# Attention over an adjacency mask, fp32 by two parts: 20 of 128 transposed probability blocks per batch taken from TensorE to VectorE squares and a DMA placement

## The reference

```python
h = jnp.maximum(_layernorm(x, axis=-1), 0.0)          # x: (16, 1024, 512)
q = (h @ Wq + bq).reshape(b, n, H, HD)                # H = 8 heads of HD = 64
k = (h @ Wk + bk).reshape(b, n, H, HD)
v = (h @ Wv + bv).reshape(b, n, H, HD)
scores = jnp.einsum('bihd,bjhd->bhij', q, k) / jnp.sqrt(jnp.float32(HD))
mask = jnp.where(adj == 0, jnp.float32(-1000000000.0), jnp.float32(0.0))
weights = jax.nn.softmax(scores + mask[None, None, :, :], axis=-1)
out = jnp.einsum('bhij,bjhd->bihd', weights, v)
return x + out.reshape(b, n, H * HD)
```

## Time and profile before

| | |
|---|---|
| median of 3 runs | 3952.41 us (3952.12 to 3953.52) |
| profiled execution, its time | 3952.87 us |
| its span | 3951.1 us |
| TensorE matmul busy | 3925.2 us, 99% |
| TensorE weight load busy | 3219.8 us, 81% |
| VectorE busy | 3109.3 us, 79% |
| ScalarE busy | 3010.7 us, 76% |
| GpSimd busy | 1389.6 us, 35% |
| granted TensorE clock | 0.999 |

### The profile page before, as it was taken

The page is one execution under the profiler, slowest core; times in us unless marked ns, Lnnn a source line. Parts: engine busy times, 40 slices in busy tenths (PEclk is TensorE's granted clock), DMA queues, the critical chain, the costliest instruction groups (busy, mean ns, idle before and its releaser), DMA issues.

```text
span 3951.1 us, 64302 instructions
## 1 busy us (share of the span) xinstructions
PE 3925.2 (99%) x21504; PEld 3219.8 (81%) x21504; DVE 3109.3 (79%) x5263; ACT 3010.7 (76%) x5386; POOL 1389.6 (35%) x1399
## 2 busy tenths in 40 slices
PE   8999999999999999999999999999999999999998
PEld 7888888888888888888888888888888888888887
DVE  7878878788787887878878788787887868878687
ACT  6877868778686886868868688686886868868687
POOL 4334333343333333333333333333333333334322
PEclk9999999999999999999999999999999999999999
DMA  6233333333323333334233342332433324324232
GB/s 208 60 88 72 88 78 67 85 79 80 83 66 83 89 70 84 73 75 95 63 84 80 68 96 65 82 84 62 96 73 75 87 61 94 80 67 90 51 76 49
DMA packets 722325, 316.44 MB, mean 80 GB/s; under 512 B 629840, under 2 KB 629840, under 8 KB 713424
## 3 DMA queue, kind: packets, MB, share of 16 engines
q1 hardware_dynamic: 722000, 312.34, 34.7%
HBM read 173.28 MB, written 38.27 MB: 54 GB/s over the span
## 4 chain that ended last, share of the span: by engine, by line
PE 92%; DVE 6%; issue 1%; ACT 1%; POOL 0%; DMA 0%; ACTq 0%; POOLq 0%; DVEq 0%
PE T L604 21%; PE misc L558 16%; PE S L589 11%; PE O L623 11%; PE S L590 11%; PE O L616 11%; PE misc L571 9%; DVE pT L909 2%; DVE S L903 1%; PE misc L537 1%; DVE bn L869 1%; DVE qB L886 1%; DVE y L928 0%; DVE qA L886 0%; ACT pT L722 0%
## 5 line engine op out<-in xcount | busy, mean ns | idle before, releaser
L909 DVE TENSOR_TENSOR pT<-T,pT 128x512 fp32r<-128x512 f32 x2048 | 1378.7, 686 | 657.1 <-ACT pT L722 651.5
L722 ACT CAST pT<-T 128x512 fp32r<-128x512 f32 x2048 | 1187.1, 590 | 412.8 <-PE T L604 326.1
L903 DVE CUSTOM_DVE_ANT_0 S<-S,mask 128x1024 f32<-128x1024 f32 x1024 | 1251.9, 1223 | 1.2 <-PE S L590 1.2
L604 PEld LDWEIGHTS T<-ident,probs 128*128 128x128 f32 x8192 | 996.9, 140 | 301.8 <-DVE pT L909 64.4
L604 PE MATMUL T<-ident,probs 128*128 128x128 f32 x8192 | 1236.5, 273 | 4.6 <-DVE pT L909 0.5
L741 ACT ACTIVATE probs<-S,negmax 128x1024 f32<-128x1024 f32 x1024 | 1150.7, 1124 | 7.0 <-DVE negmax L903 3.8
L623 PE MATMUL O<-pT,vs 128*64 128x512 f32 x2048 | 954.5, 466 | 0.2 <-DVE pT L909 0.2
L616 PE MATMUL O<-pT,vs 128*128 128x512 f32 x2048 | 816.1, 398 | 0.0
L558 PE MATMUL misc<-hT,wqk 128*128 128x512 f32 x3036 | 734.3, 391 | 0.0
L456 POOL TENSOR_TENSOR outs<-outs,oT 64x512 f32<-64x512 f32 x255 | 338.2, 1326 | 1024.4 <-DMA outs<-oT 1021.1
L558 PEld LDWEIGHTS misc<-hT,wqk 128*128 128x128 f32 x3036 | 570.0, 188 | 122.0 <-issue 0.2
(11 more groups left out here) (78 smaller groups left out, 3298.9 us busy)
## 6 DMA issues: line engine op xcount, KB each, us to landing
wqk<-wqk_split SPq DMA_DIRECT2D x63, 1024.0 KB, 6.0
xln<-in_x SPq DMA_DIRECT2D x240, 256.0 KB, 2.7
kA<-kA SPq DMA_DIRECT2D x128, 256.0 KB, 3.2
kB<-kB SPq DMA_DIRECT2D x128, 256.0 KB, 3.8
outs<-in_x SPq DMA_DIRECT2D x256, 128.0 KB, 3.6
outs<-oT SPq DMA_DIRECT2D x256, 128.0 KB, 3.6
out<-outs SPq DMA_DIRECT2D x252, 128.0 KB, 3.3
rinv_sq<-rinv_turned SPq DMA_DIRECT2D x512, 2.0 KB, 1.7
```

Of the source, the lines that this page charges most:

```text
L604: mm = pe.transpose(T[:, u % 2, i * P:(i + 1) * P], probs[:, (GB * g + i) % RING, j * P:(j + 1) * P], ident[:])
L722: act.copy(pT[:, u % PT, 0, :], T[:, u % 2, :]).then_inc(p_hi, 1)
L903: dve.tensor_tensor_reduce(S[:, s % 2, :], S[:, s % 2, :], mask[:, s % NB, :], 1.0, 3.0e38, ALU.add, ALU.min, negmax[:, s % RING:s % RING ...
L909: dve.tensor_tensor(pT[:, u % PT, 1, :], T[:, u % 2, :], pT[:, u % PT, 0, :].bitcast(F32), ALU.subtract).then_inc(p_lo, 1)
```

## The change

Twenty units of a batch are no longer turned by TensorE. Two neighbouring units make a pack: `PACKS` lists for ten packs the slot in which VectorE turns it (`at`) and its first unit (`slot`), always four later. One VectorE transpose (`turn_pack`) turns 128 x 256 columns of four ring slots in squares of 32x32 into a buffer (`squares`: part of `wv`, or `xln` for the packs from slot 121 on). As squares stay on their own 32 partitions, SP stores them to DRAM with four DMAs, one for each 32 partitions (`store_pack`, slot `at`), and one slot later, when all four have landed, loads them with two DMAs, one a unit, to the right partitions, into the place in `probs` that the unit came from (`load_pack`). `probs_hi` and `probs_low` of such a unit read `probs` in place of T, and `probs_hi` waits for the load. On ScalarE it stands behind the slot's exponential. The high half of wv that the squares overwrite is kept in DRAM (`wv_dram`) and loaded again in slot 110 (`load_wv`). The slots of the statistics of x go from (5, 7, 11, 13, 37, 39, 43, 45) to (5, 7, 11, 37, 39, 43, 69, 71). In the last batch only packs with `at` under 96 are moved.

```diff
--- before.py
+++ after.py
@@ -70,7 +70,7 @@
 HT_AT = {s: t for t, s in enumerate(HT_SLOTS)}
 NORM_AT = {s - 2: t for t, s in enumerate(HT_SLOTS)}
-STATS_SLOTS = (5, 7, 11, 13, 37, 39, 43, 45)
+STATS_SLOTS = (5, 7, 11, 37, 39, 43, 69, 71)
 STATS_AT = {s: t for t, s in enumerate(STATS_SLOTS)}
 COPY_K_AT, STORE_AT, RES_AT, WQK_AT = (8, 16), 19, 24, (21, 21, 28, 21)
@@ -88,8 +88,40 @@
 XLN = 2
 SPREAD_0 = (2, 2, 6, 6, 6, 6, 8, 8)
+PACKS = ((6, 10), (9, 13), (38, 42), (41, 45), (70, 74), (73, 77), (102, 106), (105, 109), (121, 125), (126, 130))
+TWO = 2
+WV_AT = 110
 W_ORDER = ((1, 0), (0, 0), (0, 1), (0, 2), (0, 3), (1, 1), (1, 2), (1, 3))
 XLN_USES = [len(range(r, NB, XLN)) for r in range(XLN)]
+def packs_of(b):
+    return [(k, at, slot) for k, (at, slot) in enumerate(PACKS)
+            if b < B - 1 or at < (PAIRS - 1) * PER]
+def pack_of(b, u):
+    for k, at, slot in packs_of(b):
+        if slot <= u < slot + TWO:
+            return len(PACKS) * b + k, u - slot
+    if b > 0:
+        for k, at, slot in packs_of(b - 1):
+            if slot <= u + UNITS < slot + TWO:
+                return len(PACKS) * (b - 1) + k, u + UNITS - slot
+    return None
+MOVED = [[u for u in range(UNITS) if pack_of(b, u)] for b in range(B)]
+def turned_to(n):
+    b, u = divmod(n, UNITS)
+    return n + 1 - sum(len(MOVED[i]) for i in range(b)) - len([s for s in MOVED[b] if s <= u])
 def some(n):
@@ -107,6 +139,8 @@
         rinv_dram = nc.dram_tensor("rinv_turned", [2, P, 2 * 2 * GB], F32, kind="Internal").ap()
+        turned_dram = nc.dram_tensor("probs_turned", [2, TWO * QUADS, SQ, QUADS, P], F32, kind="Internal").ap()
+        wv_dram = nc.dram_tensor("wv_low", [P, 2 * D], F32, kind="Internal").ap()
         wqk_dram = nc.dram_tensor("wqk_split", [PAIRS, P, 2 * C * 2 * P], F32, kind="Internal").ap()
@@ -120,6 +154,8 @@
         kA = sb("kA", [P, 2, N], F32R)
         qB = sb("qB", [P, 2, N], F32R)
         kB = sb("kB", [P, 2, 2, N], F32R)
+        with nc.sbuf_tensor("wv_squares", [P, TWO * QUADS, P], F32) as wv_squares:
+            pass
         wv = sb("wv", [P, 2, C, D], F32R)
         wqk = sb("wqk", [P, 2, C, 2, P], F32R)
         pT = sb("pT", [P, PT, 2, GB * P], F32R)
@@ -172,6 +208,7 @@
         w_in, adj_in = [sem(f"w_in{w}") for w in range(3)], [sem(f"adj_in{i}") for i in range(4)]
         x0_in, b_in = [sem(f"x0_in{i}") for i in range(4)], sem("b_in")
+        wv_out, wv_in = sem("wv_out"), sem("wv_in")
         wv_split, wqk_split = sem("wv_split"), sem("wqk_split")
         wqk_stored = [sem(f"wqk_stored{r}") for r in range(PAIRS)]
         w0_split, w3_split = sem("w0_split"), sem("w3_split")
@@ -191,6 +228,7 @@
         inverted, y_turned = sem("inverted"), sem("y_turned")
         o_copied, o_moved, o_summed = sem("o_copied"), sem("o_moved"), sem("o_summed")
         y_scaled, y_added = sem("y_scaled"), sem("y_added")
+        sq_turned, sq_out, sq_in = sem("sq_turned"), sem("sq_out"), [sem(f"sq_in{i}") for i in range(TWO)]
         rinv_out, rinv_in, tail_done = sem("rinv_out"), sem("rinv_in"), sem("tail_done")
@@ -203,6 +241,20 @@
             if not second:
                 return qA[:, :], kA[:, :, :]
             return qB[:, pair % 2, :], kB[:, pair % 2, :, :]
+        def probs_of(n, blocks=1):
+            g, j = n // NB, n % NB
+            at = GB * g % RING
+            return probs[:, at:at + GB, j * P:(j + blocks) * P]
+        wv_shared = wv[:, 0, 0:2, :].rearrange("p c n -> p (c n)").bitcast(F32)
+        def squares(at):
+            return wv_squares[:] if at < V_FROM else xln[:].rearrange("p t (j n) -> p (t j) n", n=P)
         def x_tile(b, t):
@@ -303,6 +355,32 @@
             for i in range(4):
                 sp.dma_start(adj_in_sb[:, 2 * i:2 * i + 2, :], adj_blocks[:, 2 * i:2 * i + 2]).then_inc(adj_in[i], 16)
+            def store_pack(b, k, at):
+                n, src = len(PACKS) * b + k, squares(at)
+                sp.wait_ge(sq_turned, n + 1)
+                if some(n - 1):
+                    for i in range(TWO):
+                        sp.wait_ge(sq_in[i], 16 * (n - 1))
+                for a in range(QUADS):
+                    dst = turned_dram[n % 2, :, :, a, :].rearrange("j c n -> c j n")
+                    sp.dma_start(dst, src[a * SQ:(a + 1) * SQ]).then_inc(sq_out, 16)
+            def load_pack(b, k, slot):
+                n = len(PACKS) * b + k
+                sp.wait_ge(sq_out, 16 * QUADS * (n + 1))
+                for i in range(TWO):
+                    src = turned_dram[n % 2, QUADS * i:QUADS * (i + 1)].rearrange("q c a n -> (q c) a n")
+                    sp.dma_start(probs_of(UNITS * b + slot + i), src).then_inc(sq_in[i], 16)
+            def load_wv(b):
+                sp.wait_ge(sq_out, 16 * QUADS * (len(PACKS) * b + len([at for at, _ in PACKS if at < V_FROM])))
+                sp.wait_ge(wv_out, 16)
+                sp.dma_start(wv_shared, wv_dram).then_inc(wv_in, 16)
             def store_wqk(r):
                 src = wqk_parts[r].rearrange("p w c l n -> p (w c l n)")
                 sp.dma_start(wqk_dram[r], src.bitcast(F32)).then_inc(wqk_stored[r], 16)
@@ -313,6 +391,8 @@
             store_wqk(1)
             sp.wait_ge(w0_split, 2)
             store_wqk(0)
+            sp.wait_ge(wv_split, 1)
+            sp.dma_start(wv_dram, wv_shared).then_inc(wv_out, 16)
             sp.wait_ge(h_turned, NB)
             for t in range(XLN):
                 load_xln(1, t)
@@ -369,6 +449,13 @@
                         if first and p < 2:
                             sp.wait_ge(wqk_stored[p + 2], 16)
                         load_wqk((p + 2) % PAIRS)
+                    for k, at, slot in packs_of(b):
+                        if u == at:
+                            store_pack(b, k, at)
+                        if u == at + 1:
+                            load_pack(b, k, slot)
+                    if u == WV_AT and not last:
+                        load_wv(b)
             body(0, first=True)
             for b in range(1, B - 1):
@@ -564,8 +651,10 @@
                 pe.wait_ge(h_lo, NB * (b + 1))
                 pe.wait_ge(*free)
-                if isinstance(b, int) and b == 0:
+                if b == 0:
                     pe.wait_ge(wv_split, 1)
+                elif j == 0:
+                    pe.wait_ge(wv_in, 16 * b)
                 parts = [(c, wl, hl) for c in range(C) for wl, hl in ((0, 0), (1, 0), (0, 1))]
                 for n, (c, wl, hl) in enumerate(parts):
                     mm = pe.matmul(bank, hT[:, hl, c, j * P:(j + 1) * P], wv[:, wl, c, :],
@@ -594,10 +683,15 @@
             def turn_probs(b, u):
                 n, g, j = UNITS * b + u, u // NB, u % NB
+                if pack_of(b, u):
+                    return
                 if j == 0:
                     pe.wait_ge(exped, GB * (GROUPS * b + g + 1))
-                if some(n - 1):
-                    pe.wait_ge(p_lo, n - 1)
+                last = n - 2
+                while last >= 0 and pack_of(*divmod(last, UNITS)):
+                    last -= 2
+                if last >= 0:
+                    pe.wait_ge(p_lo, last + 1)
                 else:
                     pe.wait_ge(v_biased, V_EARLY - 1 + n)
                 for i in range(GB):
@@ -712,20 +806,31 @@
             def probs_hi(b, u):
                 n = UNITS * b + u
-                act.wait_ge(turned, n + 1)
+                moved = pack_of(b, u)
+                if moved:
+                    act.wait_ge(sq_in[moved[1]], 16 * (moved[0] + 1))
+                else:
+                    act.wait_ge(turned, turned_to(n))
                 if n == 0:
                     act.wait_ge(wqk_stored[1], 16)
                 used = n + 1 - (PT if u >= PT - 1 else PT - 1)
                 if some(used):
                     act.wait_ge(contracted, used)
-                act.copy(pT[:, u % PT, 0, :], T[:, u % 2, :]).then_inc(p_hi, 1)
+                if moved:
+                    act.copy(pT[:, u % PT, 0, :].rearrange("p (t a r) -> p a t r", t=GB, a=QUADS),
+                             probs_of(n).rearrange("p a (t r) -> p a t r", r=SQ)).then_inc(p_hi, 1)
+                else:
+                    act.copy(pT[:, u % PT, 0, :], T[:, u % 2, :]).then_inc(p_hi, 1)
             def exponential(b, s):
                 n = SBLOCKS * b + s
                 free = NB * (GROUPS * b + s // GB - 1)
                 if some(free):
-                    act.wait_ge(turned, free)
+                    act.wait_ge(turned, turned_to(free - 1))
+                    moved = [m for m in range(free - NB, free) if pack_of(*divmod(m, UNITS))]
+                    if moved and s % GB == 0:
+                        act.wait_ge(p_lo, moved[-1] + 1)
                 if n == 0:
                     act.wait_ge(w0_split, 2)
                     act.wait_ge(wqk_split, 2)
@@ -833,12 +938,16 @@
                         copy_out(b - 1, GROUPS - 1)
                     if u > 1 and u % NB == 1:
                         copy_out(b, u // NB - 1)
```

(29 more changed lines are left out.)

## The result

| | before | after |
|---|---|---|
| median | 3952.38 us (4 runs) | 4128.55 us (4 runs, 4123 to 4141) |
| ratio | | 1.045, 95% interval 1.0425 to 1.0475: slower |
| profiled execution's span | 3951.1 us | 4139.7 us |
| granted TensorE clock, mean | 0.999 | 0.981 |

The change costs 176 us where I forecast 101 (4053, with 3920 to 4190 as the range).

The account below looks back on a forecast made before the run. It took TensorE and VectorE together as the bound in the pairs' full stretch. 3952.9 + 126 (63 pairs, 2.0 us each waiting for the DRAM round trip) - 26 beside the V projections = 4053 us; range 3920 to 4190.

Parts of the forecast that it names:

- Direction and mechanism: In pairs of heads, ScalarE's copies wait for loads of turned blocks and TensorE idles: slower, 4003 to 4180 us, chance 0.70.
- The trip, part by part: Slots 13 and 14: store issues 2.0, landing 2.5, queue wake-up 0.1, load 2.8, together 7.4 us.
- The rule R - 5.4: Each pair of heads grows by the DRAM round trip R minus 5.4 us; 2.0 us at R = 7.4.
- the date of block 14: Slot 14's high contraction started at 2049.54; a round trip of 5.6 us or less costs nothing there.
- the term 63 x 2.0: 63 pairs of heads, each 2.0 us longer from waiting for the DRAM round trip: 126 us.
- the queue as a rival: Stores stand behind copy_k and the first pack's loads: round trip 10 us or more, 4217 us and up; chance 0.06.
- The idle time: TensorE idle ahead of the two contractions, 63 x (2.0 + 1.72) = 234 us in total, busy share down to 94%.
- The first pack adds nothing: The pair's first pack, turned in slot 6, has 7.8 us for a 7.4 us trip, so adds no time.
- Beside the V projections: 60 blocks in slots 125, 126, 2, 3 have 16 us for the trip: 26 us gained, bounds 0 and 26.
- Ports: VectorE's subtraction for moved blocks reads two SBUF operands; 0 to 0.56 us a pair possible beside GpSimd, taken as 0.
- Statistics: Moving statistics of x to other slots: counted at nothing, bounded by 0.69 us less or more in a pair.
- Rival (b): TensorE stays the bound and VectorE's slack takes all: 312 x 0.43 gained, 3819 us, or half, 3886; chance 0.11.

Follow-up runs that it names:

- experiment 2: Changed kernel without the stores and loads of the turned squares, moved blocks copied unturned, VectorE still turning: 3952.05 us (0.9998 of the kernel before).
- (6): Changed kernel with the second pack of each pair of heads one slot later, blocks 14 and 15 in place of 13 and 14: 4017.93 us (1.0166).
- experiment 3: Changed kernel without the DRAM trip, VectorE's turns and the reload of wv, moved blocks copied unturned: 3952.23 us (1.0000 of the kernel before).
- experiment 4: Changed kernel plus six TensorE matmuls in each pair of heads, placed in its holes: 4104.81 us (1.0387 of the kernel before).
- experiment 9: Kernel before with only the statistics of x moved to the new slots: 3943.95 us (0.9978).
- (10): Kernel before plus only the two packs beside V projections and the new statistics slots: 3925.98 us; also one early-turned pack a pair, copied ahead of the exponential: 3920.84.
- experiment 8: Changed kernel, one pack a pair turned in slot 6, used in 13 and 14, old statistics slots: 3951.34 us; with block 14's copy ahead of the exponential: 3931.03.

## Why the prediction was right, and where it was short

- *Direction and mechanism held.* The holes are at the moved blocks' contractions, behind loads that ScalarE's copies wait for. ScalarE waited 111 us for the loads of the pairs' second packs, 1.8 us a pair, where I had 1.5 to 2. Behind the load it took 2.80 us against 2.82. Without the trip the loss is gone (experiment 2), with one slot more of time 111 us of it are (6).
- *The trip, part by part.* It took 7.08 us undisturbed against 7.4, but its parts were off both ways. From the first store's issue to the last landing it took 3.86 us (2313.54 to 2317.40) against 4.5 + 0.1, because four issues took 1.90 us and not 2.72; from the load's issue to the copy 3.20 against 2.8. That the sum came so close is in part luck.
- *The rule R - 5.4* gives 2.8, 2.8, 2.5 and 1.8 us for the trips measured in the four kinds of pair (8.2, 8.2, 7.9 and 7.2 us). The pairs without half clock were 2.6, 2.7, 2.4 and 1.8 longer. So the date of block 14 was read rightly, and the term 63 x 2.0 (126 us, measured 150) was short because the trip was longer in the first three pairs. I had 9.0 and 10 as bounds and the queue as a rival, but not in the sum.
- *The idle time* that I forecast, 234 us ahead of the two contractions, all at blocks 13 and 14, was 179 us: 115 at blocks 13 and 14 and 63 at block 10. That all holes of TensorE sum to 225 is no match, as 26 of these were there before. Work at half clock fills some of the rest: TensorE's busy time is 80 us longer than in experiment 2.
- *"The first pack adds nothing"* did not hold for its waits. Its loads leave 0.57 us after its stores have landed, behind a statistic's wait and `load_xln` on SP (2130.41), and the first of them arrives 8.1 to 8.4 us after the turn on average, 11.1 at most, not 7.4. ScalarE waits for this pack over half a microsecond in 37 of the 48 pairs that are a batch's first to third, 55 us in all, and the longest holes are of this kind. Block 10's contraction is also 0.55 us late from the new order alone, 35 us over the pairs in experiment 3; the prediction counts that order for block 14 and not for block 10. How much of this lengthens a pair, beside the clock, is not shown apart.
- *The clock was missing from the sum*, about 55 us. In the profiled execution the change cost 188 us where I forecast 101; of the 88 in between, 55 are the clock, 24 the pairs and 9 the stretch beside the V projections. (The three other runs, 171 to 178 us above before, had a granted clock of 0.985 or 0.986 in place of 0.981, so their share of the clock is smaller.) That the clock costs time is shown by experiment 4; its price a piece is read from pairs with and without, not from a run of its own. That the number came within the range, with the clock left out, is luck as well: the range was made wide for longer trips.
- *Beside the V projections* 17 to 18 us against 26. The slots 125 and 126 gave 0.47 of 0.86 us: the first pack there is used four slots after its turn, so it does not have the 16 us that I gave it, and block 125 waited 0.5 to 0.8 us for its load in most batches. The rest I did not trace.
- *Ports.* Moved subtractions took 725 ns on average against 685; 312 x 0.04 = 12 us of VectorE, with no loss that I could tell apart.
- *Statistics*: counted at nothing, worth -9 in the kernel before (experiment 9) and as much beside the V packs (10).
- *Rival (b)*, TensorE as the only bound, is further off than I gave it. Without trip and turns none of the 108 us of the pairs' blocks come through (3), but there the change's own order on ScalarE makes part of the holes. With the order undone and one pack a pair, 4 of 54 come through (8). I had VectorE's turn down as the reason; without the turns nothing changed.

## What to carry to other kernels

An engine busy for 99% of the span need not be the only bound: taking 54 us of its work away gave 4 (experiment 8). Read the stretch of the change on all engines, and ask for the date at which the next result can be there, before counting the work taken away. A result that goes out over DRAM and back costs two landings and the issues between them (7 us here, up to 11 with other transfers around), so give it that in slots, and look at what stands behind it in the in-order queue of the engine that waits. A copy moved behind a long instruction of its queue costs something in itself, 20 us here for one block a pair. Put such work where the busy engine has long pieces and the others are idle, here beside the V projections.

## What the runs showed of the hardware

A granted clock of half the rate followed holes of TensorE in 33 places, while three holes of 2.0 to 3.2 us had none behind them. The place shown came behind 3.76 us of idle time and lasted 3.4 us, in which a matmul step took 0.43 us in place of 0.23. The Trainium skill (TensorE: Matmul & The Clock Gate, Part 1) says that the engine falls to 1.2 GHz when it has been idle, and the trace agrees at this place. Landings of 256 KB loads with other transfers around them spread widely. With a load of x issued 0.4 us ahead and two copies of 256 KB from 1.3 us behind, nine of 45 took 5.8 to 6.7 us; with the copies alone all 18 took 3.1 to 3.5; with the copies moved away none took over 5.0.
